# Merged key products, transposed values, and a buffer of its own for the last rope pair

## The reference

```
xn  = layernorm(x)
qkv = xn @ w_qkv                       # 32 query heads, 8 key and 8 value heads, head size 16
xq, xk = rope(xq), rope(xk)            # r1 = x1*cos - x2*sin, r2 = x1*sin + x2*cos
scores = xq . xk / sqrt(16), causal, softmax; out = probs @ xv
x = x + out @ w_o + ffn(xn)            # ffn: (silu(xn Wg) * (xn Wu)) Wd, weights w * (su @ sv)
```

## Time and profile before

| | before |
|---|---|
| median of 3 runs | 719.05 us |
| the profiled execution | 718.95 us |
| its span | 717.2 us |
| PE busy | 687.6 us (96%) |
| PE weight loads busy | 519.9 us (72%) |
| DVE busy | 415.0 us (58%) |
| ACT busy | 293.1 us (41%) |
| POOL busy | 237.6 us (33%) |

### The profile page before, as it was taken

The page is one execution under the profiler, slowest core; times in us unless marked ns, Lnnn a source line. Parts: engine busy times, 40 slices in busy tenths (PEclk is TensorE's granted clock), DMA queues, the critical chain, the costliest instruction groups (busy, mean ns, idle before and its releaser), DMA issues. The chain is left out here.

```text
span 717.2 us, 10113 instructions
## 1 busy us (share of the span) xinstructions
PE 687.6 (96%) x3606; PEld 519.9 (72%) x3606; DVE 415.0 (58%) x982; ACT 293.1 (41%) x548; POOL 237.6 (33%) x241
## 2 busy tenths in 40 slices
PE   8997999999999999999999999879999999978998
PEld 7876666666666666666787788757888888856886
DVE  6634876776676676664377650297554554635611
ACT  4213255554555455455344232254334444332421
POOL 4465022332222222222234535233232322203443
PEclk9999799999999999999999999969999999997999
DMA  9328515323313232311155500020000100103211
GB/s 304 106 91 234 127 31 134 75 73 73 72 44 73 74 80 70 83 45 45 48 179 164 192 16 1 22 87 30 31 30 30 60 30 1 42 7 97 60 58 59
DMA packets 23147, 55.19 MB, mean 77 GB/s; under 512 B 3733, under 2 KB 4089, under 8 KB 22041
## 3 DMA queue, kind: packets, MB, share of 16 engines
q1 hardware_dynamic: 22840, 54.41, 26.5%
q10 hardware_dynamic: 256, 0.13, 0.1%
HBM read 42.86 MB, written 11.54 MB: 76 GB/s over the span
## 5 line engine op out<-in xcount | busy, mean ns | idle before, releaser
L956 DVE CUSTOM_DVE_ANT_0 bank<-bank,mask 128x512 f32<-128x512 f32 (+3 forms) x256 | 118.4, 523 | 64.1 <-PE bank L1010 63.9
L214 POOL TENSOR_TENSOR up_w_lo<-up_w_eff,up_w_hi 128x512 fp32r<-128x512 f32 x50 | 66.3, 1335 | 121.7 <-ACT up_w_hi L210 121.7
L52 PE MATMUL bank<-x0T_hi,up_w_hi 128*128 128x512 f32 x224 | 97.1, 434 | 4.8 <-DVE up_gated L280 2.5
L364 POOL TENSOR_TENSOR down_h_lo<-hidden,down_h_hi 128x512 fp32r<-128x512 f32 x50 | 65.8, 1316 | 106.6 <-ACT down_h_hi L359 106.5
L910 ACT ACTIVATE probs<-bank 128x512 f32<-128x512 f32 x160 | 85.3, 598 | 28.2 <-PE bank L1032 25.4
L54 PE MATMUL bank<-x0T_lo,up_w_hi 128*128 128x512 f32 x224 | 89.9, 401 | 0.0
L53 PE MATMUL bank<-x0T_hi,up_w_lo 128*128 128x512 f32 x224 | 89.5, 399 | 0.0
L52 PE MATMUL bank<-down_w_hi,down_h_hi 128*128 128x512 f32 x200 | 79.5, 398 | 1.1 <-DVE down_w_lo L349 0.7
L875 POOL TENSOR_SCALAR_AFFINE_SELECT probs<-probs 128x512 f32<-128x512 f32 x64 | 40.0, 637 | 122.1 <-ACT probs L910 122.1
L53 PE MATMUL bank<-down_w_hi,down_h_lo 128*128 128x512 f32 x200 | 78.9, 395 | 0.0
L54 PE MATMUL bank<-down_w_lo,down_h_hi 128*128 128x512 f32 x200 | 78.9, 394 | 0.0
(11 more groups left out here) (146 smaller groups left out, 1275.2 us busy)
## 6 DMA issues: line engine op xcount, KB each, us to landing
w_raw<-in_w_gate_up SPq DMA_DIRECT2D x25, 512.0 KB, 4.2
w_raw<-in_w_down SPq DMA_DIRECT2D x25, 256.0 KB, 2.7
q_stack<-q_hi SPq DMA_DIRECT2D x32, 128.0 KB, 3.5
att<-att_T SPq DMA_DIRECT2D x16, 256.0 KB, 2.1
q_hi<-rope_hi SPq DMA_DIRECT2D x8, 256.0 KB
q_lo<-rope_lo SPq DMA_DIRECT2D x8, 256.0 KB
q_stack<-q_lo SPq DMA_DIRECT2D x16, 128.0 KB, 3.7
attention_or_xn<-att SPq DMA_DIRECT2D x16, 128.0 KB
```

The costliest lines, as they stand in the source:

```text
L52: pe.matmul(out, w_hi, m_hi, start=first, stop=False, skip_group_check=True)
L214: pool.tensor_tensor(self.half(self.w_lo[:, o % 2], k), self.half(self.w_eff, k), f32(self.half(self.w_hi[:, o % 2], k)), ALU.subtract).th ...
L364: pool.tensor_tensor(self.h_lo[:, k % 2, :], self.hid[:, o, b * S:(b + 1) * S], f32(self.h_hi[:, k % 2, :]), ALU.subtract).then_inc(self.h ...
L956: dve.tensor_tensor_reduce(out=own, in0=own, in1=e.mask[:, S - w:S], scale=1.0, scalar=NEG, op0=ALU.add, op1=ALU.max, accum_out=rmax[:, i, ...
```

## The change

Seven edits, all in the front:

- A key pair is one product of 128 output columns (x1 rows on partitions 0 to 63, x2 rows on 64 to 127) in one bank, 12 matmuls instead of 24; DVE reads its halves through `half_of`.
- Values are made with the value columns on the partitions and all 512 tokens of a batch as the moving side (`value_rows`, 12 matmuls of 128 x 512), copied by ACT to `v_row` (in the space of the raw QKV weights), and transposed back by PE in four float32 transposes (`turn_values`); ACT then places them in `v`. Batch 0's rows stand between pairs 2 and 3, its transposes behind pair 3; batch 1's rows stand between pairs 4 and 5, its transposes behind pair 5.
- The second batch's four tiles are transposed in one group behind pair 1, into banks 4 to 7, instead of two behind pair 0 and two behind pair 1; their high and low parts stand together on ACT and DVE.
- The factors of chunk 0 go from behind pair 4 to behind pair 3, and with them DVE's combine, ACT's high parts and POOL's low parts.
- `stack_lo` of the first part of `lr` goes from behind pair 3's products to behind pair 2's.
- DVE's `rest(3)` goes behind pair 4's products, `rest(4)` behind pair 5's; `rest(5)` goes to the end of POOL's list.
- Pair 5 is rounded into the first down projection's buffers `h_hi` and `h_lo` (free until step 214), so its rounding doesn't wait for the stores of pair 3.

```diff
-        rot_hi = sb("rope_hi", [P, 2, 2, S], F32R)
-        rot_lo = sb("rope_lo", [P, 2, 2, S], F32R)
+        slots_hi = sb("rope_hi", [P, 2, 2, S], F32R)
+        slots_lo = sb("rope_lo", [P, 2, 2, S], F32R)
+        rot_hi = [slots_hi[:, n % 2] for n in range(5)] + [e.rope_spare[0][:, :, :]]
+        rot_lo = [slots_lo[:, n % 2] for n in range(5)] + [e.rope_spare[1][:, :, :]]
...
-        norm = Norm(nc, ctx, "norm0", x_sb, x_sb, lambda t: (x_loaded[t], 16), lambda t: e.bank[4 + (t if t < NJ else t % 2)], e.ident,
+        norm = Norm(nc, ctx, "norm0", x_sb, x_sb, lambda t: (x_loaded[t], 16), lambda t: e.bank[4 + t % NJ], e.ident,
...
+        v_row = w_raw[:, :, :].rearrange("p c n -> p (c n)")[:, 4 * S:6 * S].rearrange("p (b s) -> p b s", b=B)
...
-        cols = [(0, KV * FR), (P, 3 * P), (2 * P, 4 * P)]
+        cols = [None, ((P, 2 * P), (3 * P, 4 * P)), ((2 * P, 3 * P), (4 * P, 5 * P))]
+
+        def half_of(n, part):
+
+            bank = 2 * (n % 2)
+            return e.bank[bank][KV * FR * part:KV * FR * (part + 1), :] if pairs[n][1] == 0 else e.bank[bank + part][:, :]
...
             def rest(n):
                 R = rows[pairs[n][1]]
                 pool.wait_ge(hi_ready, n + 1)
-                if n >= 2:
-                    pool.wait_ge(stored[n % 2], 64 * (n // 2))
-                pool.tensor_tensor(rot_lo[0:R, n % 2], rot[0:R, n % 2], f32(rot_hi[0:R, n % 2]), ALU.subtract).then_inc(lo_ready, 1)
+                if n == 2:
+                    pool.wait_ge(stored[0], 64)
+                if n == 5:
+                    pool.wait_ge(lo_ready, 5)
+                pool.tensor_tensor(rot_lo[n][0:R], rot[0:R, n % 2], f32(rot_hi[n][0:R]), ALU.subtract).then_inc(lo_ready, 1)
...
-                if n == 4:
+                if n == 3:
                     for k in range(2):
                         up.pool_lo(pool, 0, k)
+            rest(5)
...
+            def copy_rows(b):
+                act.wait_ge(v_mm, b + 1)
+                act.activation(v_row[:, b, :], e.bank[6 + b][:, :], ACT.Copy).then_inc(v_rows, 1)
...
+            def place_values(b):
+                act.wait_ge(norm.transposed, NT + b + 1)
...
+            for t in range(NJ, NT):
+                norm.act_hi(act, t)
             for n, (b, k) in enumerate(pairs):
-                for t in HI_BEFORE.get(n, ()):
-                    norm.act_hi(act, t)
                 if n == 1:
                     stack_hi(act, e.lr0, lr_raw, slice(0, LR0_FIRST), lr_in, 16, lr_hi)
+                if n == 2:
+                    copy_rows(0)
+                if n == 3:
+                    place_values(0)
+                    for factor in range(2):
+                        up.act_hi(act, 0, factor)
+                if n == 4:
+                    copy_rows(1)
                 act.wait_ge(summed, 2 * (n + 1))
-                if n >= 2:
+                if 2 <= n <= 4:
                     act.wait_ge(stored[n % 2], 64 * (n // 2))
-                act.activation(rot_hi[0:rows[k], n % 2], rot[0:rows[k], n % 2], ACT.Copy).then_inc(hi_ready, 1)
+                act.activation(rot_hi[n][0:rows[k]], rot[0:rows[k], n % 2], ACT.Copy).then_inc(hi_ready, 1)
                 if n == 4:
-                    for k in range(2):
-                        up.act_hi(act, 0, k)
...
+                    place_values(1)
...
+                dve.tensor_tensor(rot_lo[n][0:R], rot[0:R, n % 2], f32(rot_hi[n][0:R]), ALU.subtract).then_inc(lo_ready, 1)
...
             for n, (b, k) in enumerate(pairs):
-                if n >= 4:
-                    rest(n - 1)
                 dve.wait_ge(pair_mm, n + 1)
...
-                    dve.scalar_tensor_tensor(out=prod[0:R, n % 2, m, :], in0=e.bank[2 * (n % 2) + src][0:R, :],
+                    dve.scalar_tensor_tensor(out=prod[0:R, n % 2, m, :], in0=half_of(n, src),
...
+                if n == 1:
+                    for t in range(NJ, NT):
+                        norm.dve_lo(dve, t)
+                if n == 2:
+                    stack_lo(dve, e.lr0, lr_raw, slice(0, D), slice(D, LR0_FIRST), lr_hi, 1, lr_lo)
                 if n == 3:
-                    stack_lo(dve, e.lr0, lr_raw, slice(0, D), slice(D, LR0_FIRST), lr_hi, 1, lr_lo)
-                if n == 4:
                     for k in range(2):
                         up.dve_combine(dve, 0, k)
-            rest(len(pairs) - 1)
+                if n == 4:
+                    rest(3)
+            rest(4)
...
+            def pair(n):
+                b, k = pairs[n]
+                if n >= 2:
+                    pe.wait_ge(products, 4 * (n - 1))
+                for r in range(1 if k == 0 else 2):
+                    own = slice(0, P) if k == 0 else slice(*cols[k][r])
...
+            def value_rows(b):
+                own = slice(5 * P, 6 * P)
+                for c in range(NC):
+                    last = three_pass(pe, e.bank[6 + b][:, :], w_hi[:, c, own], w_lo[:, c, own],
+                                      e.xT_hi[:, c, b * S:(b + 1) * S], e.xT_lo[:, c, b * S:(b + 1) * S], c == 0, c == NC - 1)
+                last.then_inc(v_mm, 1)
+
+            def turn_values(b):
+                pe.wait_ge(v_rows, b + 1)
                 for j in range(NJ):
-                    tok = slice(b * S + j * P, b * S + (j + 1) * P)
-                    for c in range(NC):
-                        last = three_pass(pe, e.bank[6 + b][:, j * P:(j + 1) * P], e.xT_hi[:, c, tok], e.xT_lo[:, c, tok],
-                                          w_hi[:, c, 5 * P:6 * P], w_lo[:, c, 5 * P:6 * P], c == 0, c == NC - 1)
-                last.then_inc(v_mm, 1)
+                    last = pe.transpose(e.bank[6 + b][:, j * P:(j + 1) * P], v_row[:, b, j * P:(j + 1) * P], e.ident[:, :])
+                last.then_inc(norm.transposed, 1)
 
...
+            pair(0)
+            pair(1)
+            for t in range(NJ, NT):
+                norm.pe_transpose(pe, t, t - NJ)
+            pair(2)
+            pe.wait_ge(norm.lo, NT)
+            value_rows(0)
+            pair(3)
+            turn_values(0)
+            pe.wait_ge(lr_lo, 2)
+            for factor in range(2):
+                up.pe_factor(pe, 0, factor)
+            pair(4)
+            value_rows(1)
+            pair(5)
+            turn_values(1)
...
+                e.rope_spare = small[1:]
```

More of the change, by code:

```diff
@@ L495, in store_pair @@
                         sp.dma_start(dst[part][b, r, :, h0:h0 + nh, :].rearrange("f h s -> h f s"),
-                                     f32(src[0:rows[k], n % 2, r, :])).then_inc(stored[n % 2], 16)
+                                     f32(src[n][0:rows[k], r, :])).then_inc(stored[n % 2], 16)
             for n in range(3):
@@ L624, in tensor @@
             pe.wait_ge(e.ident_in, 16)
-            def products_of(b):
-                pe.wait_ge(norm.lo, NJ * (b + 1))
-                if b == 0:
-                    pe.wait_ge(w_lo_ready, 1)
-                for n in range(3 * b, 3 * b + 3):
-                    k = pairs[n][1]
-                    if n >= 2:
-                        pe.wait_ge(products, 4 * (n - 1))
-                    for r in range(2):
-                        c0 = cols[k][r]
-                        for c in range(NC):
-                            if (n, r) == (1, 0) and c < NC - 1:
-                                pe.wait_ge(w_lo_ready, c + 2)
-                            if (n, r) == (1, 0) and c == NC - 1:
-                                pe.wait_ge(w_lo_last, 1)
-                            last = three_pass(pe, e.bank[2 * (n % 2) + r][0:rows[k], :], w_hi[:, c, c0:c0 + rows[k]],
-                                              w_lo[:, c, c0:c0 + rows[k]], e.xT_hi[:, c, b * S:(b + 1) * S],
-                                              e.xT_lo[:, c, b * S:(b + 1) * S], c == 0, c == NC - 1)
-                    last.then_inc(pair_mm, 1)
-                    if n == 4:
-                        pe.wait_ge(lr_lo, 2)
-                        pe.wait_ge(norm.lo, NT)
-                        for factor in range(2):
-                            up.pe_factor(pe, 0, factor)
-                    for t in TRANSPOSE_AFTER.get(n, ()):
-                        norm.pe_transpose(pe, t, t - NJ if t < NJ + 2 else t - 2)
-                for j in range(NJ):
-                    tok = slice(b * S + j * P, b * S + (j + 1) * P)
-                    for c in range(NC):
-                        last = three_pass(pe, e.bank[6 + b][:, j * P:(j + 1) * P], e.xT_hi[:, c, tok], e.xT_lo[:, c, tok],
-                                          w_hi[:, c, 5 * P:6 * P], w_lo[:, c, 5 * P:6 * P], c == 0, c == NC - 1)
-                last.then_inc(v_mm, 1)
@@ new lines, in pair @@
+            def pair(n):
[5 more added lines that the diff above has]
+                    for c in range(NC):
+                        if (n, r) == (1, 0) and c < NC - 1:
+                            pe.wait_ge(w_lo_ready, c + 2)
+                        if (n, r) == (1, 0) and c == NC - 1:
+                            pe.wait_ge(w_lo_last, 1)
```

(18 more changed lines are left out.)

13 lines of the change are left out of this document (3 added, 10 removed).

## The result

The first timing gave 712.7 us as the median of four of its six runs (709.79 the lowest), since the other two were disturbed: one, the profiled one, took 940 us with 0.65 of the clock granted nearly from end to end, the other 3683 us. The kernel before took 717.01 (6 runs): ratio 0.9932, interval 0.9903 to 0.9961. A second timing, of 6 and 11 runs, gave 711.50 against 717.08: ratio 0.9919, interval 0.9896 to 0.9943, or 5.8 us less (4.1 to 7.5). The forecast was 704.5, the range 702 to 711; both medians lie above it.

What follows compares the result with a forecast made beforehand. PE, busy 96% of the span, was taken as the bound. 9.7 us less PE work and shorter waits bring PE's restart 12.2 us earlier, step 16 14.4 with the clock kept: 718.95 - 14.4 = 704.5, range 702 to 711.

Steps and rivals of the forecast that it cites:

- PE work and its waits: Front up to the up projection: merged keys and new values save 9.7 us; first up product ready at 50.4.
- the place named as the one without room: Factor (1, 1), three steps into the up projection: needs pair 5's products at 52.35 against 52.5.
- The chain to G: Pair 5's products, sums, rounding and table load up to G, the first gate's start, forecast at 59.5.
- the rule quoted from the Trainium skill: Two-input SBUF operations on DVE and GpSimd exclude each other for whole instructions; by it G would be 0.7 later.
- My estimate by scaling: Pair 5's POOL sums beside DVE's low part of pair 4: 0.45 us added, scaled from an earlier row.
- Stack 0: Group 0's stack on SP's queue: lands 56.6, PE asks at 55.75, a 0.9 us wait that doesn't delay the first gate.
- rival 1: Clock falls again in the stretch around the first gate: gain 12.2 instead of 14.4 us, 706.8; chance 0.22.
- the first gap of 2.30 us: PE idle until 62.65 in the kernel before; the clock stayed at 1.00 until 71, taken as evidence against a fall.
- the last of the sum: Behind step 16, forecast 14.4 us earlier: remaining waits are on the kernel's own work and move along, giving 704.5.
- Its last sign of being wrong: Listed sign of failure: a gain at 75 us that is gone at the end of the span.
- the lump of several waits: Case of several waits that together leave 5 us or less of gain; chance 0.05.

Runs made afterwards that it cites:

- keys_old_late: Changed kernel with stack 3 held until the first minus-maximum row landed and key products unmerged again (24 matmuls a pair): 711.8 us, ratio 0.9929 to before.
- filled_gap: Changed kernel with 24 identity products on PE ahead of step 8 to keep the clock up: 713.3 us, ratio 0.9926 to before.
- all_three: Changed kernel with tanh table loaded early, gap filled with 12 identity products and stack 3 held back: 703.3 us, ratio 0.9794 to before.
- early_table: Changed kernel with a one-column tanh on ACT ahead of pair 5's rounding, so the table loads early: 712.0 us, ratio 0.9918 to before.
- late_stack3: Changed kernel with SP holding stack 3 and the weights behind it until the first minus-maximum row landed: 708.5 us, ratio 0.9856 to before.
- before_late: Kernel before the change, with stack 3 held until the first minus-maximum row landed: 715.9 us, ratio 0.9985 to before.
- late_weights: Changed kernel with only the weights of chunk 3 (512 KB) held until the first minus-maximum row landed: 709.2 us, ratio 0.9895 to before.
- table_late: Changed kernel with tanh table loaded early and stack 3 held back, without identity products: 705.1 us, ratio 0.9830 to before.
- before_filled: Kernel before the change, with 18 identity products on PE in the gap ahead of step 8: 719.7 us, ratio 1.0035 to before.

## Why the prediction was wrong, step by step

**PE work and its waits: right.** First up product forecast at 50.4 with a front that starts at 20.57; measured 51.61 with a start at 21.83, so 50.35. The wait for `up_w_lo` is gone, and the factor that takes bank 2 waited 0.16, the place named as the one without room.

**The chain to G: right, 0.8 short.** Forecast 38.93 behind the first rope product, measured 39.76. Pair 5's four rope products took 2.84 instead of 2.45: on the merged key bank they start 0.71 apart instead of 0.60. With the key products unmerged (keys_old_late) the four took 2.48 again, so this is a cost of the merge, which the prediction had put at nothing. Its two sums took 3.45 instead of 3.0, because `rope_sum` at 54.06 ran 2.21 us while DVE's low part of pair 4 ran to 55.11. Here the rule quoted from the Trainium skill, SBUF — State Buffer, section "SBUF: two separate sides" (a whole instruction is locked out), was the better one: of the 1.05 us of overlap the sum lost 0.9. At 47.94 it goes the other way, DVE's `rope_lo` takes 2.24 instead of 1.2 us while POOL's `up_w_lo` runs to 49.1. My estimate by scaling was half of it, and it rested on a misread row: the 2.38 us of DVE's `lr` work are two operations that had themselves waited for POOL's sums (a wider one, 32x768, takes 0.95 us alone). The two therefore hold less work than 2.38 us, and the 0.9 us that the sums lost beside them is a larger share of it than I took.

**Stack 0: right in place, and nothing.** Last issue at 54.09 (forecast 52.6, plus the late start), landed within 3.3 us, and the burst went at 57.37 without the 0.9 us of wait that stood in the sum.

**The clock: rival 1 came in.** The gap ahead of step 8 was 3.34 us, the clock fell, and the stretch from the first gate to the second took 12.4 us. With the clock kept it takes 10.8 to 10.9 (filled_gap, all_three, early_table) where the forecast had 10.6 (its 11.2 run to the end of the second gate, 0.6 later). What a low clock costs here goes by how long it lasts: 10.65 us from gate to gate with 3.4 us of it (late_stack3, before_late), 11.9 with 6.8 (late_weights, table_late), 12.45 with 10.2, each in one or two profiles. The clock fell in all three profiles of the changed front that have the unfilled gap of 3.2 to 3.4 us, so the chance of 0.22 was too small. Before, I took the first gap of 2.30 us as evidence that such a gap leaves the clock alone; two other profiles of the same front have it fall right there.

**The failed step** is the last of the sum: "From there the kernel's waits are on its own work and move along." PE came 10 us closer to SP's queue, but the queue itself moved only 5.8 (weights of chunk 3 issued at 71.90 instead of 77.68). It is bound by its own issues: from the first of stack 0 it issues without a pause, 20.05 us to the weights of chunk 3 against 20.81 before, and stack 0 moved by only 5.0 (51.85 instead of 56.87). The DMAs' share is 0.94 from 57 to 79 us. So the small DMA on ACT's queue that carries the row now goes out 2.5 us behind 512 KB of weights instead of 7 us behind them, and took 4.9 us to land; where SP's loads were held it took 1.85. The prediction listed this queue, but only asked of it when stack 0 lands. Its last sign of being wrong, a gain at 75 us that is gone at the end of the span, names the outcome; among the rivals only the lump of several waits, at 0.05, comes near it. The ledger of the profiled pair, from 14.4 to 7.0: late start 1.3 (input DMAs, no part of the change), chain 0.8, low clock 1.8, row with the second fall of the clock 3, smaller waits for rows further on 0.5. The two profiled executions differ by 7.4 us in time and the medians by 5.6, since the profiled one of before lies 1.9 us above its median. Of the 8.8 us that are missing, the row is thus the largest term, but not most of it.

Shown by experiment: that the row's DMA sets a floor near 79 us (three issue times, one landing), that holding the loads removes it and does nothing for the kernel before, and that undoing any one of the three parts of the change costs 4.6 to 5.1 us of the front. Not shown: why low stretches last 3 us in one execution and 10 in another, which is worth up to 2 us. In the changed front the two kernels with a filled gap kept the clock, one profile each; in before_filled it fell at an earlier gap that wasn't filled.

## What to carry to other kernels

When a stage is pulled forward by 10 us, lay the DMA queue beside it on the same axis and ask of every small transfer that the compute will want what it will now share the DMAs with, issued before it or just behind it; a chain that was 7 us clear of a bulk load may not be afterwards. A gain that vanishes at a fixed time, whatever is saved ahead of it, is a floor set by something that did not move: three variants with three issue times and one landing time find it faster than any sum. And before a clock term goes into a forecast, one profile of the baseline is not enough: the same front had it low for 3 us and for 10. Work put into a gap to keep the clock has to be measured against the gap: here 18 products took 4.18 us and held up what came next.

## What the runs showed of the hardware

- A 4 KB DMA issued on ACT's queue landed 1.85 us after its issue with the loads on SP's queue held (late_stack3), 3.8 us after it with six stack DMAs issued ahead (late_weights), and 4.9, 7.4 and 8.2 us after it where 512 KB of weights stood on SP's queue too, issued 2.5 us before it, 0.9 us before it and 1.0 us behind it.
- POOL and DVE, both reading two SBUF operands, took turns by whole instructions in the rows above: 2.21 and 2.29 us for a sum that takes 1.28 alone, 2.24 for a low part that takes 1.2.
- Four rope products read from one bank, two of them from partitions 64 to 127, took 2.84 us; from two banks 2.47 (before) and 2.48 (keys_old_late).
- The granted clock fell behind an idle gap of 1.8 us (table_late) and of 2.30 us (before_late, before_filled), and stayed up behind one of 1.9 us (early_table) and one of 2.30 us (before). Low stretches of 3.4, 6.8 and 10.2 us gave 10.65, 11.9 and 12.45 to 12.8 us from the first gate to the second.
- A float32 identity product of 128x128 shows as two matmuls and took 0.23 us (12, 18 and 24 of them took 2.84, 4.18 and 5.52 us).
- The start of the changed front's rope products lay between 20.90 and 23.37 us from one profiled execution to another; in the latest, DVE waited 2.13 us for an input DMA at 16.84.
